# Weights in PSUM, and ScalarE scales the accumulator for half of the units of the first attention

## The chip, the cores and the metric

One core of one Trainium2 chip runs the whole program. The metric is the device time in microseconds (us). The engines are named as in the profile: PE (TensorE), PEld (its weight load), DVE (VectorE), ACT (ScalarE), POOL (GpSimd), SP (SyncE).

## The reference

A node feature matrix `x` (6250 nodes, 256 features) passes through four layers, each with a layer norm ahead of it and a residual around it: a graph attention with 4 heads, a mixture of 6 experts (2 chosen per node), a graph attention with 1 head, and a dense mixture of 8 experts. There are 106250 edges, sorted by their target `dst`. An attention computes:

```python
e = leaky_relu(a_src[src] + a_dst[dst], 0.2)     # per edge and head
m = segment_max(e, dst)
e = exp(e - m[dst])
alpha = e / segment_sum(e, dst)[dst]
out = segment_sum(alpha[:, :, None] * h[src], dst)
```

The dense mixture computes softmax shares of 8 experts for each node, three 256 x 256 layers per expert, and the sum of the experts' outputs weighted with the shares.

## The kernel before, in words

`attention(l, acc, sc)` runs once for each attention layer (`l` is 0 and 1; `H` heads, 4 and 1). Edges are cut into units of 256 (`UE`), each with targets in one tile of 125 nodes; a slot is 8 units (`U`), 16 columns of 128 edges (`Q`). There are 58 slots. The loop over slots is written out, five stages deep: in turn `i`, POOL gathers the rows of slot `i`, DVE builds the incidence of slot `i`, slot `i-1` has its maxima found, slot `i-2` has its weights computed and its units 0 to 3 summed, and slot `i-3` has its units 4 to 7 summed. Buffers `G` and `MB` have a ring of 3 slots.

POOL issues one indirect gather (L682) for each of the 16 columns; before a unit's two it waits until PE has summed that unit of three slots back (`summed`).

PE (from L686), per turn: two transposes (L729, L730) when the rows of slot `i-1` are there; `sums(3,4..6)`; two `spread` (L700, targets spread over partitions); `sums(3,7)`; the transposes of the selection (L741, L742); `sums(2,0..1)`; the product at L752; two more `spread`; `sums(2,2..3)`; the product at L765. A `sums(k,u)` (L715) is two matrix products of a unit's incidence with its rows, into one of four PSUM banks in turn; it waits until DVE has taken the sum four units back (`acc`).

ACT (from L771), per turn: copy of `LT` (L820), `place(0)` (L786, two operations that wait for `spread`), `hit(0)` (L798), the exponential of the weights (L828), `place(1)`, the selection copy (L835), `hit(1)`, eight small copies (L845), `place` and `hit` 2 and 3, and the exponential of the maxima's change, `c1` (L862). `lower` (L800) scales a tile of the accumulator `acc` with `c1`, one operation per head; it does so only for units that are not in `FUSED`, and before the change every unit is in it.

DVE (from L866), per turn: `dloc` (L965), logits and weights of slot `i-2` between the scan of slot `i-1` (L974 to L996, with `te` at L991), `scale(0)`, `merge(3,4)`, `merge(3,5)`, the rest of the selection (L1002), `scale(1)`, `merge(3,6)`, `merge(3,7)`, L1009 to L1018, `scale(2)`, the maxima (L1023 to L1056), `scale(3)`, and then `merge(2,0..3)` with four `incidence` (L952) among them. `scale` in layer 0 multiplies the gathered rows with the weights (L935); in layer 1 it multiplies the incidence with them (L938). `merge` of a unit in `FUSED` is one operation per head (L920): accumulator tile times `c1` plus PE's sum; of another unit it is one plain addition over all heads (L914), after `lowered`. Consecutive units may have the same tile, so both `merge` and `lower` wait for the sum of the unit before (`acc`).

`dense_experts` (L1070) runs over groups of 250 nodes (25 of them) and 8 experts `e`. PE does `layer2` of the expert before, `layer1` of this one, `layer3` of the one before; at `e == 5` it then transposes the shares of the next group (`turn_shares`, L1152), which waits for `cw`. DVE adds each expert's output to `X` (`collect`, L1360, after `layer3`) and computes the next group's shares: `shares` at `e == 4`, `normal_shares` (L1335 to L1341, makes `cw`) at `e == 5`, behind `collect`.

Of the kernel before, what the change touches and what calls it, by code (L numbers as in the profile page):

```python
# [18 lines left out]
F32 = mybir.dt.float32  # L19
I32 = mybir.dt.int32  # L20
BF16 = mybir.dt.bfloat16
ALU = mybir.AluOpType
# [3 lines left out]
P = 128  # L26
N = 6250
D = 256
TN = 125
# [4 lines left out]
C = 2  # L34
UE = P * C
UNITS = (E + (UE - 1) * NT) // UE
U = 8
# [20 lines left out]
HEADS = (4, 1)  # L58
FUSED = ((0, 1, 2, 3, 4, 5, 6, 7), (0, 1, 2, 3, 4, 5, 6, 7))
SLOPES = (0.2, 0.01)  # L60
# [7 lines left out]
def build(nc, a, out):  # L68
    ctx = ExitStack()
    with ctx:  # L70
        def sb(name, shape, dt=F32, scope=ctx):
            return scope.enter_context(nc.sbuf_tensor(name, shape, dt))
# [472 lines left out]
        def attention(l, acc, sc):  # L545
# [14 lines left out]
            if l == 1:  # L560
                qe = sb(p + "qe", [P, RING, Q], F32, sc)
                b = sb(p + "b", [P, RING, Q, H], F32, sc)
                wt = sb(p + "wt", [P, RING, Q, H], F32, sc)
                M = sb(p + "M", [P, MR, CP, TN], F32, sc)
# [35 lines left out]

            def sum_bank(u):
                return bank[(4, 5, 1, 7)[u % 4]]

# [29 lines left out]
            with nc.Block() as block:  # L633
# [53 lines left out]
                def _(pe):  # L687
                    def slot(i, r, t):
# [14 lines left out]
                        def sums(k, u):  # L703

                            if not has(i, k):
                                return
                            rk = (r - k) % RING
                            if u % 2 == 0:
                                pe.wait_ge(S(p + "scaled"), i * V - k * V + (u // 2 + 1))
                            if u >= 4 or late(i, k + 1):  # L710
                                after(pe, p + "acc", i * U - k * U + (u - 3))
                            for c in range(C):
                                q = u * C + c
                                left = MB[:, rk, q, :] if l == 0 else M[:, turn(r, k, u // 2), q % CP, :]
                                mm_ = nc.tensor.matmul(sum_bank(u)[0:TN, 0:HW], left, G[:, rk, q, :], start=(c == 0), stop=(c == C - 1))  # L715
                            mm_.then_inc(S(p + "summed"), 1)
# [26 lines left out]
                        sums(2, 0)  # L743
                        sums(2, 1)
                        if one:

                            pe.wait_ge(S(p + "MB"), i * V)
                            pe.wait_ge(S(p + "RS"), i)
                            if late(i, 2):
                                after(pe, p + "top", i - 1)  # L750
                            for q in range(Q):
                                mm_ = nc.tensor.matmul(V_ps[:, q * 3 * H:(q + 1) * 3 * H], hot(r1, q), RS[:, :, q, :], start=True, stop=True)  # L752
                            mm_.then_inc(S(p + "V"), 1)
                        spread(2)
                        spread(3)
                        sums(2, 2)
                        sums(2, 3)
                        if one:

                            pe.wait_ge(S(p + "rhs"), i)  # L760
                            pe.wait_ge(S(p + "MT"), i * V)
                            if late(i, 2):
                                after(pe, p + "xs", i - 1)
                            for q in range(Q):
                                mm_ = nc.tensor.matmul(Xe_ps[:, q * 6 * H:(q + 1) * 6 * H], MT[:, turn(r, 1, q // CP), q % CP, :],  # L765
                                                       rhs[:, q // C, :, 0:KM:KM - 1, :], start=True, stop=True)
                            mm_.then_inc(S(p + "Xe"), 1)
                    run(pe, slot)

                @block.scalar  # L770
                def _(act):  # L771
                    tile_regs = [[act.alloc_register(f"{p}atile{k}_{u}") for u in range(U)] for k in range(RING)]

                    def slot(i, r, t):
# [40 lines left out]
                        if one:  # L815
# [4 lines left out]
                            nc.scalar.copy(LT[:, :], rowT_ps[:, P:2 * P]).then_inc(S(p + "LT"), 1)  # L820
                        place(0)
                        lower(3, U - 2)
                        hit(0)
                        if two:

                            act.wait_ge(S(p + "te"), i - 1)
                            to = wt[:, r2, :, :] if l == 1 else G[:, r2, :, :].rearrange("p q (h w) -> p q h w", h=H)[:, :, :, DH]
                            nc.scalar.activation(to, te[:, :, :], ACT.Exp).then_inc(S(p + "w"), 1)  # L828
                        lower(3, U - 1)
                        place(1)  # L830
# [6 lines left out]
                        if one:  # L837
# [9 lines left out]
                            ins.then_inc(S(p + "ad_in"), 1)  # L847
                        lower(2, 0)
                        place(2)
                        lower(2, 1)  # L850
                        hit(2)
                        place(3)
                        lower(2, 2)
                        hit(3)
                        lower(2, 3)
                        lower(2, 4)
                        lower(2, 5)
                        if one:
# [7 lines left out]
                def _(v):  # L866
# [32 lines left out]
                    def slot(i, r, t):  # L899
# [3 lines left out]
                        def merge(k, u):  # L903
# [6 lines left out]
                            if u in own:  # L910
                                v.wait_ge(S(p + "lowered"), scaled_acc(k, i, u))
                                at = acc[:, bass.ds(j * HW, HW)]
                                ins = nc.vector.tensor_tensor(at, at, sum_bank(u)[0:TN, 0:HW], ALU.add)
                            else:  # L914
# [3 lines left out]
                                for h in range(H):  # L918
                                    at = acc[:, bass.ds(j * HW + h * W, W)]
                                    ins = nc.vector.scalar_tensor_tensor(at, at, c1[:, rk, u, h:h + 1], sum_bank(u)[0:TN, h * W:(h + 1) * W],  # L920
                                                                         ALU.mult, ALU.add)
                            ins.then_inc(S(p + "acc"), 1)

                        def scale(v_):
# [8 lines left out]
                            if l == 0:  # L933
                                g = G[:, r2, at, :].rearrange("p q (h w) -> p (q h) w", h=H)
                                ins = nc.vector.tensor_tensor(g[:, :, 0:DH], g[:, :, 0:DH], g[:, :, DH:W].broadcast_to([P, CP * H, DH]), ALU.mult)  # L935
                            else:
                                after(v, p + "summed", (i * V - 2 * V + v_) * 2 - 2 * MR + 2)
                                ins = nc.vector.tensor_tensor(M[:, turn(r, 2, v_), :, :], MB[:, r2, at, :], wt[:, r2, at, :].broadcast_to([P, CP, TN]), ALU.mult)  # L938
                            ins.then_inc(S(p + "scaled"), 1)
# [130 lines left out]
        def dense_experts(acc, sc):  # L1070
# [39 lines left out]
            with nc.Block() as block:  # L1110
# [173 lines left out]
                def _(v):  # L1284
# [655 lines left out]
```

## Time and profile before

| what | us |
|---|---|
| median of 3 runs | 4750.13 (4743.02 to 4752.10) |
| the profiled execution | 4749.81 |
| its span | 4748.1 |
| PE, DVE, ACT, POOL busy | 3401.8, 2688.4, 1539.8, 2214.1 |
| first attention: first to last gather | 184.6 to 1519.7 |
| second attention: first to last gather | 2346.5 to 3537.0 |
| dense experts | about 3590 to 4748 |

The span is one execution on the chip, from its first to its last instruction; the profiled execution's own time is 1.7 us above it. "Busy" is the time in which an engine had an instruction under way. Idle time of an engine matters only where it lies on the path that sets the end of a stage, so the stages are read one by one.

### The profile page before, as it was taken

The numbers are of one execution on the slowest core, as the hardware profiler recorded it, in microseconds if no ns is written. First come the engines' busy times: TensorE is split into PE (matmuls) and PEld (weight loads), VectorE is DVE, ScalarE is ACT, GpSimd is POOL, SyncE is SP. The second block draws the span as 40 slices with busy tenths as digits, with TensorE's granted clock in tenths as the row PEclk, the third lists the DMA queues.
The fourth block names the chain that finished last, engine by engine and source line by source line (L and its number), as shares of the span: only waits on it lengthen the run. The fifth ranks groups of instructions, "written<-read, shape, count | busy, mean of one in ns | idle before, by whom it ended". The sixth has DMA issues, their size and how long they took to land. (4 is left out here: it accounts for less than half of the span.)

```text
span 4748.1 us, 73243 instructions
## 1 busy us (share of the span) xinstructions
PE 3401.8 (72%) x16240; PEld 2620.6 (55%) x16241; DVE 2688.4 (57%) x8451; ACT 1539.8 (32%) x4325; POOL 2214.1 (47%) x2095
## 2 busy tenths in 40 slices
PE   5267667665776768884467766666558999999999
PEld 3144444444444557773245444444436888888887
DVE  7478888788887775555455556655555412222121
ACT  2233333333332203331133333333333333333333
POOL 0377777777776013227577777777750000000000
PEclk9676776777667559996667788888878999999999
DMA  3333333333336214443344444444461000000000
GB/s 100 80 95 93 94 94 95 95 94 94 93 94 78 90 34 158 157 132 102 95 105 106 106 105 105 106 106 105 106 84 57 7 5 6 4 6 6 4 7 7
DMA packets 382578, 369.58 MB, mean 78 GB/s; under 512 B 249324, under 2 KB 309388, under 8 KB 382242
## 3 DMA queue, kind: packets, MB, share of 16 engines
q0 software_dynamic: 107072, 272.84, 23.1%
q1 hardware_dynamic: 272774, 92.39, 8.1%
q14 instruction: 244, 2.00, 0.1%
q8 instruction: 92, 1.51, 0.1%
q10 hardware_dynamic: 2396, 0.84, 0.1%
HBM read 324.13 MB, written 41.59 MB: 77 GB/s over the span
## 5 line engine op out<-in xcount | busy, mean ns | idle before, releaser
L682 POOL DMA_INDIRECT g_G<-rows,g_pack x1856 | 1959.6, 1056 | 782.1 <-issue 496.4
L715 PE MATMUL bank<-g_G,g_MB 128*125 128x260 f32 x1856 | 718.4, 551 | 145.4 <-DVE acc L920 143.2
L786 ACT ACTIVATE g_mt_d<-bank,unode 125x256 bf16<-125x256 f32 x928 | 384.9, 465 | 898.5 <-PE bank L700 898.4
L715 PE MATMUL bank<-g_G,g_M 128*125 128x257 f32 x1856 | 612.8, 489 | 84.9 <-DVE acc L920 84.1
L715 PEld LDWEIGHTS bank<-g_G,g_MB 128*125 128x125 f32 x1856 | 486.4, 277 | 337.3 <-DVE g_G L935 152.0
L920 DVE SCALAR_TENSOR_TENSOR acc<-acc,g_c,bank 125x65 f32 (+1 forms) x2320 | 619.0, 316 | 88.9 <-DVE acc L920 83.3
L1360 DVE SCALAR_TENSOR_TENSOR X<-bank,e_cw,X 125x256 f32 (+1 forms) x400 | 175.2, 479 | 842.9 <-PE bank L1186 842.9
L1256 ACT ACTIVATE e_h<-bank,e_bi_c,e_sc_c 128x250 f32<-128x250 f32 x800 | 404.2, 556 | 556.8 <-PE bank L1177 419.7
L715 PEld LDWEIGHTS bank<-g_G,g_M 128*125 128x125 f32 x1856 | 441.4, 249 | 223.8 <-DVE g_M L938 89.6
L935 DVE TENSOR_TENSOR g_G<-g_G 128x1024 f32<-128x1024 f32 x232 | 283.1, 1221 | 191.4 <-ACT g_G L828 191.4
L1186 PE MATMUL bank<-e_w,e_h 128*125 128x256 f32 x1600 | 377.9, 379 | 3.1 <-ACT e_h L1256 3.1
L1177 PE MATMUL bank<-e_h,e_w 128*128 128x250 f32 x1600 | 376.6, 377 | 1.2 <-ACT e_h L1256 1.2
L1168 PE MATMUL bank<-e_xnT,e_w 128*128 128x250 f32 x1600 | 371.9, 374 | 0.0
L798 ACT ACTIVATE g_MT<-g_mt_d,ones 125x512 bf16<-125x512 bf16 x464 | 335.6, 723 | 11.3
L1186 PEld LDWEIGHTS bank<-e_w,e_h 128*125 128x125 f32 x1600 | 299.3, 187 | 47.2 <-ACT e_h L1256 3.9
L1168 PEld LDWEIGHTS bank<-e_xnT,e_w 128*128 128x128 f32 x1600 | 303.7, 190 | 36.3 <-issue 0.7
L1177 PEld LDWEIGHTS bank<-e_h,e_w 128*128 128x128 f32 x1600 | 296.1, 190 | 42.7 <-issue 8.0
L938 DVE TENSOR_TENSOR g_M<-g_MB,g_wt 128x500 f32<-128x500 bf16 x232 | 155.7, 671 | 288.8 <-PE bank L715 282.3
L952 DVE TENSOR_TENSOR g_MB<-iota_b,g_dloc 128x500 f32<-128x500 bf16 (+1 forms) x464 | 301.9, 673 | 0.1
L820 ACT COPY g_LT<-bank 64x128 f32<-64x128 f32 (+1 forms) x116 | 29.8, 257 | 804.9 <-PE bank L730 804.9
L729 PE MATMUL bank<-ident,g_b 128*16 128x128 f32 x58 | 21.6, 372 | 336.0 <-DVE g_dloc L965 265.7
L729 PE MATMUL bank<-ident,g_G 128*64 128x128 f32 x58 | 23.5, 405 | 317.7 <-DMA g_G<-rows,g_pack 317.7
(302 smaller groups left out, 4194.6 us busy)
## 6 DMA issues: line engine op xcount, KB each, us to landing
g_G<-rows,g_pack POOLq DMA_INDIRECT x1856
acc<-in_edge_attr SPq DMA_DIRECT2D x50, 531.2 KB
g_pack<-edge_pack SPq DMA_DIRECT2D x928, 2.0 KB
g_drow<-edge_dst SPq DMA_DIRECT2D x928, 1.0 KB
expert_out<-x_y SPq DMA_DIRECT2D x54, 256.0 KB
g_qe<-edge_q SPq DMA_DIRECT2D x464, 1.0 KB
rows<-acc SPq DMA_DIRECT2D x25, 253.9 KB
rows<-n_T SPq DMA_DIRECT2D x25, 251.0 KB
```

The source lines that it names most:

```text
L682: nc.gpsimd.indirect_dma_start(G[:, r, q, :], None, rows_d[l], bass.IndirectOffsetOnAxis(ap=pack[:, r, q, 0:1], axis=0)).then_inc(S(p + f" ...
L715: mm_ = nc.tensor.matmul(sum_bank(u)[0:TN, 0:HW], left, G[:, rk, q, :], start=(c == 0), stop=(c == C - 1))
L786: ins = nc.scalar.activation(mt_d[:, v_ % 2, k * C:(k + 1) * C, :], bank[2 + v_ % 2][0:TN, k * UE:(k + 1) * UE].rearrange("p (e c) -> p c ...
L798: nc.scalar.activation(MT[:, turn(r, 1, v_), :, :], mt_d[:, v_ % 2, :, :], ACT.Relu, bias=ones[0:TN, 0:1], scale=-1.0).then_inc(S(p + "MT" ...
L920: ins = nc.vector.scalar_tensor_tensor(at, at, c1[:, rk, u, h:h + 1], sum_bank(u)[0:TN, h * W:(h + 1) * W], ALU.mult, ALU.add)
L935: ins = nc.vector.tensor_tensor(g[:, :, 0:DH], g[:, :, 0:DH], g[:, :, DH:W].broadcast_to([P, CP * H, DH]), ALU.mult)
L952: nc.vector.tensor_tensor(MB[:, r, at, :], iota_b[:, 0:TN].unsqueeze(1).broadcast_to([P, CP, TN]), dloc[:, r, at, 0:1].broadcast_to([P, CP ...
L1168: mm = nc.tensor.matmul(bank[m][:, 0:GN], w1[:, e, k, m * P:(m + 1) * P], xnT[:, r, k, :], start=(k == 0), stop=(k == 1))
L1177: mm = nc.tensor.matmul(bank[2 + m][:, 0:GN], w2[:, e, k, m * P:(m + 1) * P], h1[:, k, :], start=(k == 0), stop=(k == 1))
L1186: mm = nc.tensor.matmul(bank[4 + u][0:TN, 0:D], h2[:, e % 2, k, u * TN:(u + 1) * TN], w3[:, e, k, :], start=(k == 0), stop=(k == 1))
L1256: ins = nc.scalar.activation((h1 if q == 0 else h2[:, e % 2, :, :])[:, m, :], bank[2 * q + m][:, 0:GN], ACT.Relu, bias=bi_c[:, q, m, e:e + ...
L1360: ins = nc.vector.scalar_tensor_tensor(xt, bank[4 + u][0:TN, 0:D], cw[:, r, u, e:e + 1], xt, ALU.mult, ALU.add)
```

## The change

- `FUSED` for layer 0 becomes units 0 to 3. Units 4 to 7 are scaled by ACT (`lower`, four operations of 65 columns) and added by DVE (one operation of 260 columns).
- The exponentials of the weights go into PSUM bank 7 (`w_ps`), and `scale` reads them there in both layers. Layer 0 also still writes them to column 64 of each head in `G`. The tile `wt` is gone.
- `sums` uses three banks in turn (4, 5, 1) in place of four, and waits for the sum three units back.
- PE's order: `sums(2,1)` moves behind the product at L752, `sums(2,3)` behind the one at L765.
- ACT's order: the exponential comes first after `LT`, then `lower(3,4)`, `place(0)`, `hit(0)`, `lower(3,5)`, `place(1)`, ...; `lower(3,6)` and `lower(3,7)` come behind the eight copies, ahead of `place(2)`. The calls `lower(2,...)`, which did nothing, are gone.
- In the dense experts `normal_shares` comes ahead of `collect` at `e == 5`.

```diff
-FUSED = ((0, 1, 2, 3, 4, 5, 6, 7), (0, 1, 2, 3, 4, 5, 6, 7))
+FUSED = (tuple(range(4)), tuple(range(8)))
...
-                wt = sb(p + "wt", [P, RING, Q, H], F32, sc)
...
-            def sum_bank(u):
-                return bank[(4, 5, 1, 7)[u % 4]]
+            w_ps = bank[7][:, 0:QH].rearrange("p (q h) -> p q h", h=H)
+
+            def sum_bank(r, k, u):
+
+                return bank[(4, 5, 1)[((r - k) % RING * U + u) % 3]]
...
-                            if u >= 4 or late(i, k + 1):
-                                after(pe, p + "acc", i * U - k * U + (u - 3))
+                            if u >= 3 or late(i, k + 1):
+                                after(pe, p + "acc", i * U - k * U + (u - 2))
...
                         sums(2, 0)
-                        sums(2, 1)
                         if one:
...
                             mm_.then_inc(S(p + "V"), 1)
+                        sums(2, 1)
                         spread(2)
                         spread(3)
                         sums(2, 2)
-                        sums(2, 3)
                         if one:
...
                             mm_.then_inc(S(p + "Xe"), 1)
+                        sums(2, 3)
...
+                        if two:
+
+                            act.wait_ge(S(p + "te"), i - 1)
+                            if l == 0:
+                                nc.scalar.activation(G[:, r2, :, :].rearrange("p q (h w) -> p q h w", h=H)[:, :, :, DH], te[:, :, :], ACT.Exp)
+                            nc.scalar.activation(w_ps, te[:, :, :], ACT.Exp).then_inc(S(p + "w"), 1)
+                        lower(3, 4)
                         place(0)
-                        lower(3, U - 2)
                         hit(0)
-                        if two:
-
-                            act.wait_ge(S(p + "te"), i - 1)
-                            to = wt[:, r2, :, :] if l == 1 else G[:, r2, :, :].rearrange("p q (h w) -> p q h w", h=H)[:, :, :, DH]
-                            nc.scalar.activation(to, te[:, :, :], ACT.Exp).then_inc(S(p + "w"), 1)
-                        lower(3, U - 1)
+                        lower(3, 5)
                         place(1)
...
-                        lower(2, 0)
+                        lower(3, 6)
+                        lower(3, 7)
                         place(2)
-                        lower(2, 1)
                         hit(2)
...
-                                ins = nc.vector.tensor_tensor(g[:, :, 0:DH], g[:, :, 0:DH], g[:, :, DH:W].broadcast_to([P, CP * H, DH]), ALU.mult)
+                                w = w_ps[:, at, :].rearrange("p q h -> p (q h)").unsqueeze(2).broadcast_to([P, CP * H, DH])
+                                ins = nc.vector.tensor_tensor(g[:, :, 0:DH], g[:, :, 0:DH], w, ALU.mult)
...
-                                ins = nc.vector.tensor_tensor(M[:, turn(r, 2, v_), :, :], MB[:, r2, at, :], wt[:, r2, at, :].broadcast_to([P, CP, TN]), ALU.mult)
+                                ins = nc.vector.tensor_tensor(M[:, turn(r, 2, v_), :, :], MB[:, r2, at, :], w_ps[:, at, :].broadcast_to([P, CP, TN]), ALU.mult)
...
                         for e in range(NX):
+                            if follows(i) and e == 5:
+                                normal_shares(i + 1, 1 - r)
                             if e or late(i, 1):
                                 collect(i if e else i - 1, r if e else 1 - r, i * NX + e - 1, (e - 1) % NX)
...
-                                if e == 5:
-                                    normal_shares(i + 1, 1 - r)
```

## Rows read from the trace of the kernel before

**Rows 1.** The page, part 1: busy us (share of the span) x instructions.
```profile
PE 3401.8 (72%) x16240; PEld 2620.6 (55%) x16241; DVE 2688.4 (57%) x8451; ACT 1539.8 (32%) x4325; POOL 2214.1 (47%) x2095
```

**Rows 2.** Busy time by stretch; columns in the first line; first attention, second, dense experts.
```profile
core 0: us, PE busy (x) PEld busy (x) DVE busy (x) ACT busy (x) POOL busy (x), PEclk, DMA share, GB/s
400.00:1400.00 1000.00, 664.03 (x3127) 450.14 (x3126) 813.61 (x2818) 328.26 (x1037) 788.98 (x693) 0.71 0.38 94
2500.00:3500.00 1000.00, 635.93 (x3515) 454.70 (x3516) 602.89 (x2057) 353.77 (x1172) 761.89 (x781) 0.81 0.45 105
3700.00:4700.00 1000.00, 962.96 (x4613) 835.99 (x4612) 217.91 (x593) 381.68 (x772) 0.00 (x0) 1.00 0.02 6
```

**Rows 3.** PE's waits, 3700 to 4700 us: waited for, us in total, times, longest us.
```profile
PE bank L1152 <- DVE e_cw L1341: 35.0, 22, 1.6
PE bank L1186 <- ACT e_h L1256: 2.0, 1, 2.0
```

**Rows 4.** POOL by line, 400 to 1400, then 2500 to 3500: busy, mean ns | idle before.
```profile
L682 POOL DMA_INDIRECT g_G<-rows,g_pack x693 | 789.9, 1140 | 211.3 <-issue 181.4 <-PE bank L715 29.9
...
L682 POOL DMA_INDIRECT g_G<-rows,g_pack x781 | 762.3, 976 | 238.2 <-issue 210.4 <-PE bank L715 27.8
```

**Rows 5.** The order of time, 813 to 819 us: start us, us, engine line op.
```profile
813.74 0.86 DVE L920 SCALAR_TENSOR_TENSOR acc<-acc,g_c,bank 125x65 f32 x4 [0.24 <-DVE acc L920]
813.86 0.95 POOL L682 DMA_INDIRECT g_G<-rows,g_pack  x1 [0.30 <-issue]
...
818.14 1.22 DVE L935 TENSOR_TENSOR g_G<-g_G 128x1024 f32<-128x1024 f32 x1
...
818.25 1.93 POOL L682 DMA_INDIRECT g_G<-rows,g_pack  x1 [0.30 <-issue]
```

**Rows 6.** The same for POOL: first and last of 154 lengthened gathers of that kind.
```profile
400.94 1.57 POOL L682 DMA_INDIRECT g_G<-rows,g_pack  x1 [0.30 <-issue]
...
1397.44 1.93 POOL L682 DMA_INDIRECT g_G<-rows,g_pack  x1 [0.30 <-issue]
```

**Rows 7.** DVE by line and form, whole span: busy us, mean ns | idle before.
```profile
L1883 DVE TENSOR_TENSOR x_y<-bank,xbo 128x512 f32<-128x512 f32 x54 | 37.0, 686 | 33.8 <-PE bank L1828 33.3 <-issue 0.4
...
L1526 DVE TENSOR_TENSOR r_y<-acc,r_den 125x256 f32 x40 | 15.2, 422 | 4.0 <-issue 3.3
```

**Rows 8.** DVE by line, 400 to 1400 us.
```profile
L935 DVE TENSOR_TENSOR g_G<-g_G 128x1024 f32<-128x1024 f32 x174 | 212.4, 1221 | 139.9 <-ACT g_G L828 139.9
L952 DVE TENSOR_TENSOR g_MB<-iota_b,g_dloc 128x500 f32<-128x500 bf16 x172 | 112.0, 672 | 0.0
```

**Rows 9.** The order of time of one slot, 807 to 829 us.
```profile
807.41 0.22 DVE L965 TENSOR_TENSOR g_dloc<-g_pack,ubase 128x64 f32<-128x64 f32 x1
...
808.78 0.23 DVE L991 TENSOR_TENSOR g_te<-g_xs 128x64 f32<-128x64 f32 x1
...
811.18 0.30 ACT L828 ACTIVATE g_G<-g_te 128x64 f32<-128x64 f32 x1
...
811.51 1.23 DVE L935 TENSOR_TENSOR g_G<-g_G 128x1024 f32<-128x1024 f32 x1 [1.85 <-ACT g_G L828]
...
817.65 0.35 DVE L1009 TENSOR_REDUCE g_adz<-g_rhs 125x64 f32<-125x192 bf16 x1
...
829.04 0.22 DVE L965 TENSOR_TENSOR g_dloc<-g_pack,ubase 128x64 f32<-128x64 f32 x1
```

**Rows 10.** ACT by line and form, whole span.
```profile
L1256 ACT ACTIVATE e_h<-bank,e_bi_c,e_sc_c 128x250 f32<-128x250 f32 x800 | 404.2, 556 | 556.8 <-PE bank L1177 419.7 <-PE bank L1168 137.1
...
L1501 ACT ACTIVATE r_rhT<-bank,r_br 128x250 f32<-128x250 f32 x25 | 11.7, 470 | 49.2 <-PE bank L1471 49.2
```

**Rows 11.** ACT by line, 400 to 1400 us.
```profile
L786 ACT ACTIVATE g_mt_d<-bank,unode 125x256 bf16<-125x256 f32 x348 | 144.3, 465 | 377.4 <-PE bank L700 377.4
L798 ACT ACTIVATE g_MT<-g_mt_d,ones 125x512 bf16<-125x512 bf16 x173 | 125.4, 725 | 4.2
L845 ACT COPY g_rhs<-g_tab 125x24 bf16 x344 | 42.5, 216 | 0.0
...
L835 ACT CAST g_RS<-bank 128x128 bf16<-128x128 f32 x43 | 11.2, 261 | 0.0
```

**Rows 12.** DVE by line, 2500 to 3500 us.
```profile
L938 DVE TENSOR_TENSOR g_M<-g_MB,g_wt 128x500 f32<-128x500 bf16 x196 | 131.5, 671 | 250.8 <-PE bank L715 250.8
```

More of the change, by code:

```diff
@@ L714, in sums @@
                                 left = MB[:, rk, q, :] if l == 0 else M[:, turn(r, k, u // 2), q % CP, :]
-                                mm_ = nc.tensor.matmul(sum_bank(u)[0:TN, 0:HW], left, G[:, rk, q, :], start=(c == 0), stop=(c == C - 1))
+                                mm_ = nc.tensor.matmul(sum_bank(r, k, u)[0:TN, 0:HW], left, G[:, rk, q, :], start=(c == 0), stop=(c == C - 1))
                             mm_.then_inc(S(p + "summed"), 1)
@@ L820, in slot @@
                             nc.scalar.copy(LT[:, :], rowT_ps[:, P:2 * P]).then_inc(S(p + "LT"), 1)
-                        place(0)
-                        lower(3, U - 2)
-                        hit(0)
                         if two:
                             act.wait_ge(S(p + "te"), i - 1)
-                            to = wt[:, r2, :, :] if l == 1 else G[:, r2, :, :].rearrange("p q (h w) -> p q h w", h=H)[:, :, :, DH]
-                            nc.scalar.activation(to, te[:, :, :], ACT.Exp).then_inc(S(p + "w"), 1)
-                        lower(3, U - 1)
+                            if l == 0:
+                                nc.scalar.activation(G[:, r2, :, :].rearrange("p q (h w) -> p q h w", h=H)[:, :, :, DH], te[:, :, :], ACT.Exp)
+                            nc.scalar.activation(w_ps, te[:, :, :], ACT.Exp).then_inc(S(p + "w"), 1)
+                        lower(3, 4)
+                        place(0)
+                        hit(0)
+                        lower(3, 5)
                         place(1)
@@ L847, in slot @@
                             ins.then_inc(S(p + "ad_in"), 1)
-                        lower(2, 0)
+                        lower(3, 6)
+                        lower(3, 7)
                         place(2)
-                        lower(2, 1)
                         hit(2)
                         place(3)
-                        lower(2, 2)
                         hit(3)
-                        lower(2, 3)
-                        lower(2, 4)
-                        lower(2, 5)
                         if one:
@@ L912, in merge @@
                                 at = acc[:, bass.ds(j * HW, HW)]
-                                ins = nc.vector.tensor_tensor(at, at, sum_bank(u)[0:TN, 0:HW], ALU.add)
+                                ins = nc.vector.tensor_tensor(at, at, sum_bank(r, k, u)[0:TN, 0:HW], ALU.add)
                             else:
@@ L919, in merge @@
                                     at = acc[:, bass.ds(j * HW + h * W, W)]
-                                    ins = nc.vector.scalar_tensor_tensor(at, at, c1[:, rk, u, h:h + 1], sum_bank(u)[0:TN, h * W:(h + 1) * W],
+                                    ins = nc.vector.scalar_tensor_tensor(at, at, c1[:, rk, u, h:h + 1], sum_bank(r, k, u)[0:TN, h * W:(h + 1) * W],
                                                                          ALU.mult, ALU.add)
```

## The prediction

> **What bounds the kernel now.** I read the page first. No engine is busy over the whole span: PE is at 72%, DVE at 57%, POOL at 47% [rows 1]. So I asked for three stretches of 1000 us, one inside each stage that the diff touches: first attention, second attention, dense experts [rows 2].
>
> In the dense experts PE is busy 963 of 1000 us at full granted clock: that stage is PE, and each idle us of PE there is a us of the kernel. Its waits have one large entry, the transpose of the shares at L1152, which waits 1.6 us for `cw` once per group of 250 nodes, 22 times in the stretch, 35.0 us [rows 3].
>
> In both attentions POOL is the bound. It is busy 789 and 762 us, and the rest is the 0.30 us before each gather: 693 gathers with 211 us before them, 781 with 238 us, which fills both stretches [rows 4]. A slot has 16 gathers, so a slot takes 1000 x 16 / 693 = 23.1 us in the first and 1000 x 16 / 781 = 20.5 us in the second. (Cut by PE's row transposes, the first has 43.35 slots per 1000 us; I use 23.07.) The gather is the same instruction in both, yet means 1.14 us in one and 0.98 us in the other. The order of time shows why. A gather that begins during the scaled sum L920 takes 0.95 us. One that begins 0.11 us into the scaling L935 takes 1.93 us: it ends 0.82 us after L935 does [rows 5]. I laid all 692 gathers that start in the stretch against the DVE operation under way at their start. Of 167 in an L935, 154 are longer than 0.98 us, together 95 us above the 0.95 floor (the first and last of them are [rows 6]); of 72 in an L952 all 72, together 37 us; of 184 in an L920 none. L935 and L952 have two tensor inputs in SBUF; L920 has its second one in PSUM. In the second attention the same count gives 15 us for L938 and 7 us for L952.
>
> The Trainium skill (SBUF — State Buffer, Who interferes with whom) says that a DVE instruction with two SBUF inputs contends with a GpSimd instruction that reads SBUF and that the later one blocks, and it infers elsewhere in that section that `tensor_tensor` does not stall descriptor generation. The rows here agree with the first sentence and not with the second. By the second, the PSUM operand would free nothing; that is rival 3 below.
>
> **Part 1, weights in PSUM, first attention.** Four L935 per slot read the weight from PSUM. By the L920 rows this frees POOL: 95 us per 43.35 slots = 2.2 us per slot. POOL's own limit becomes 23.07 - 2.2 = 20.9 us. The scaling itself should cost the same: 512 columns with a PSUM operand take 686 ns (L1883) [rows 7], 500 with both in SBUF 672 ns (L952) [rows 8]. The exponential is now done twice (once into column 64 of each head, for the sums' weight column, and once into PSUM); the second costs about 0.2 us on ACT (0.30 us, less the 0.09 by which ACT's operations overlap) [rows 9].
>
> **Part 2, exponential ahead.** DVE waits for the exponential 139.9 us in 43 slots, 3.23 us each [rows 8], because ACT places it behind `place(0)` and `hit(0)`, which wait for PE. `te` is ready 1.6 us after the slot's first DVE operation (807.41 to 808.78 + 0.23) and L935 starts at 811.51 [rows 9]. Now it comes first: `w` is there at about 1.6 + 0.5 = 2.1, and DVE reaches `scale(0)` at 2.24 anyway. This wait goes to zero. It was slack under POOL's bound, so it is no gain by itself; it is room.
>
> **Part 3, hand-offs between ACT and DVE.** Units 4 to 7 of a slot: DVE's four scaled sums of 65 columns become one sum of 260, and ACT scales before it. `lower(3,u)` waits for the sum of unit u-1 and the sum of u waits for `lower(3,u)`, so the two engines take turns. Price of one `lower`: nearest is an ACTIVATE with a scale taken from a tile. L1256 (250 columns, scale and bias tiles) means 556 ns and L1501 (250 columns, bias tile alone) 470 ns [rows 10], so the scale tile adds 0.09 us. L786 at 256 columns is busy 144.3 / 348 = 0.415 us each, a pair 0.83 us, its second starting 0.37 us behind the first [rows 11]; less 191 columns at about 1 ns that is 0.17, with the tile 0.26 us between starts, and 0.35 us for the last. Four heads: 3 x 0.26 + 0.35 = 1.13 us, and 1.04 until ACT's next starts. Without the 0.09 it would be 0.77; I take 1.13, because L1256 and L1501 differ in that alone. The sum of 260 is 0.43 us by L1526 (256 columns, 422 ns) [rows 7]. ACT's other pieces: `place` 0.84, `hit` 0.72 (0.64 until the next starts), the eight copies 42.5 / 43 = 0.99, the selection copy 0.26 [rows 11].
>
> ACT's order from the start of a slot (DVE's L965 = 0): `w` starts at 1.84; lower 4 from 2.05; place(0) 3.09; hit(0) 3.96; lower 5 4.60 to 5.73; place(1) 5.64; selection copy 6.39; hit(1) 6.56; copies 7.20; lower 6 8.10 to 9.23; DVE's sum of unit 6 9.26 to 9.69; lower 7 9.72 to 10.85; DVE's sum of unit 7 10.88 to 11.31. DVE's L1009 follows at 11.25. From there nothing in the slot changes: L1009 at 817.65 to the next slot's L965 at 829.04 is 11.39 us [rows 9]. The slot by this chain is 22.6 us. In between DVE idles some 3.5 us, which part 2 has made room for; its work falls only by about 4 x 0.4 us (0.86 for four scaled sums [rows 5] against 0.43). So the bound passes from POOL (20.9) to the turn-taking chain (22.6): 58 slots x (23.07 - 22.6) = **27 us**. With `lower` at 0.77 us the four of them take 1.4 us less: 21.2, or 108 us.
>
> **Part 4, PE's order and three banks.** Sums of a slot now use three banks in turn, so each waits for the sum three units back, and bank 7 holds the weights. `sums(3,7)` now waits for DVE's unit 4, at about 3.9, and the selection transpose is queued behind it: ready at about 5.9, before ACT is free to copy it (6.39). `sums(2,1)` waits for unit 6 (9.7), `sums(2,2)` for unit 7, `sums(2,3)` for unit 0 of the next slot back, which is why it moved behind the transposed product at L765. PE has 664 / 43.35 = 15.3 us of work per slot [rows 2] against 22.6; next slot's first transpose can start at about 19.5 of this slot, its first spread ends near 2.5, before place(0) needs it at 3.1. I cost this at nothing; the cover is 0.6 us. Were PE a fifth slower in the some 6 us before its first spread, place(0) would come 0.6 us late, and about half of that would land on each slot (PE's own start moves with it): +0.3 us a slot, 17 us. POOL waits for `summed` of three slots back, and the latest of these now has 6 us or more in hand.
>
> **Part 5, second attention.** L938 gets its PSUM operand: its share of the lengthening is 15 us per 49 slots, 0.3 us per slot, 18 us in 58. No `lower` there. DVE has idle time to give (it waits 250.8 us before L938 in the stretch [rows 12]). But L952 is then reached some 0.8 us earlier in the slot, against a fixed rhythm of gathers of 1.25 us, and now happens to miss most of them: at the rate of the first attention (37 us in 43 slots) it would take 0.85 us per slot rather than 0.14. So -18 to +23 us; I take **-5**.
>
> **Part 6, dense experts.** The three small operations behind `cw` move ahead of the accumulation that waits for L1186. Their input `ex` is ready by then (a whole layer pass of PE, about 4 us, lies between). The transpose at L1152 waits for nothing: 24 groups x 1.59 = **38 us**; nothing else of PE's waits there is over 2 us [rows 3]. PE then is 100% busy at a clock that is already full.
>
> **Sum.** 4749.8 (the profiled run; span 4748.1) - 27 - 5 - 38 = 4680; the median of the runs, 4750.1, is 0.3 above the profiled run, so **4680 us**.
>
> **Rivals.** (1) Turns cheaper than priced: `lower` at 0.77 us, so the chain is 21.2 and POOL's 20.9 nearly shows: 4750 - 108 - 38 - 5 = 4599. For: 65 columns are short and L845's small copies start 0.12 us apart. Against: the pair L1256/L1501. (2) Turns dearer, the slower side: the four scalings of a unit do not overlap (4 x 0.35 = 1.4, that is +0.27 each for four) and each of seven hand-offs takes 0.12 us instead of 0.03: 22.6 + 1.08 + 0.63 = 24.3 us a slot, +72 us, so 4750 + 72 - 38 - 5 = 4779. It decides from a slot of 23.07 + 43/58 = 23.8 us on. For: they read and write the same tile at an address from a register, and no row shows that on ACT. Against: L786's pairs overlap, and DVE started 0.03 us after ACT's end at 811.48 [rows 9]. (3) The PSUM operand does not free POOL: the lengthening stays, POOL stays at 23.07, and only part 6 is left: 4712. Against: 184 gathers in L920.
>
> **Chances.** Forecast (4650 to 4740, with the second attention going either way) 0.55, rival 1 0.20, rival 3 0.13, rival 2 0.12. The range 4590 to 4750 leaves out rival 2 and rival 1 with the second attention at its best. What a measurement tells from no change is about 0.2%, 9.5 us. Faster needs under 4740.6: 0.84. Within: 0.06, the near side of rival 2. Slower: 0.10.
>
> **What the next profile would show.** Gathers that start in L935 and L938 at 0.95 us; the L935 wait on the exponential gone; L920 split into scaled sums of 65 and plain sums of 260 near 0.43 us; ACT's new group at about 0.29 us busy each; DVE waiting on ACT before the sums of units 5, 6 and 7, 3 to 4 us per slot; POOL with real waits on L715, busy near 75%; L1152 without a wait. I am wrong if POOL is still saturated in the first attention, if ACT's four scalings are far from 1.1 us, or if PE waits before L700 or L741.

## The result, and the profile after

The changed kernel takes 4666.8 us (median of 4 runs, 4660.5 to 4670.5), the kernel before 4747.9 us (4 runs, 4743.0 to 4752.1). The ratio is 0.983, 95% interval 0.981 to 0.985: 1.7% faster. The forecast was 4680 us, with 4590 to 4750 as its range. The profiled execution took 4670.5 us, its span is 4668.8.

The same three stretches as [rows 2], columns as there:

```profile
400.00:1400.00 1000.00, 703.82 (x3207) 453.60 (x3205) 757.38 (x2373) 515.77 (x1817) 708.97 (x712) 0.67 0.39 97
2500.00:3500.00 1000.00, 654.04 (x3509) 427.70 (x3508) 597.06 (x2041) 357.80 (x1172) 757.75 (x777) 0.75 0.47 105
3650.00:4650.00 1000.00, 998.00 (x4791) 872.60 (x4791) 229.36 (x615) 396.20 (x803) 0.00 (x0) 1.00 0.02 6
```

In the first attention POOL is busy 709 us rather than 789, ACT 516 rather than 328. The second is nearly what it was. In the dense experts PE went from 963 to 998 us at full granted clock.

POOL by line, in the first and then the second attention (compare [rows 4]); and PE's largest wait in the dense experts (compare [rows 3]):

```profile
L684 POOL DMA_INDIRECT g_G<-rows,g_pack x712 | 709.3, 996 | 291.0 <-issue 182.2 <-PE bank L717 108.8
...
L684 POOL DMA_INDIRECT g_G<-rows,g_pack x777 | 757.8, 975 | 239.6 <-issue 180.4 <-PE bank L717 59.2
```

```profile
PE bank L1186 <- ACT e_h L1256: 2.0, 1, 2.0
```

A gather of the first attention now means 996 ns instead of 1140, and POOL has begun to wait for PE: 291 us idle before 712 gathers, where 0.30 us each would be 214. It is no longer the bound there: a slot in this stretch takes 1000 x 16 / 712 = 22.47 us, where it took 23.09 (693 gathers). In the second attention almost nothing moved (976 to 975 ns). PE's wait at L1152 is gone.

Where the time went, by the start of the first and the last gather of each attention in the order of time. "Lengthened" is the sum of what the 928 gathers of an attention took above 0.95 us; "a slot" is the row above it divided by 58:

| stretch | before, us | after, us | difference |
|---|---|---|---|
| first attention, first to last gather | 1335.1 | 1289.7 | -45.4 |
| of it a slot | 23.02 | 22.24 | -0.78 |
| lengthened there | 173 | 47 | |
| from there to the second attention's first gather | 826.8 | 832.4 | +5.7 |
| second attention, first to last gather | 1190.5 | 1189.6 | -0.9 |
| lengthened there | 27 | 27 | |
| last gather to the end | 1211.1 | 1172.4 | -38.7 |

The last gather isn't the end of an attention: its rows still have to be summed. The first DVE operation behind the last sum, before and then after:

```profile
1573.45 0.34 DVE L1515 TENSOR_SCALAR r_den<-acc 125x200 f32<-125x200 f32 x1 [1.12 <-PEq L88]
...
1533.92 0.34 DVE L1515 TENSOR_SCALAR r_den<-acc 125x200 f32<-125x200 f32 x1 [1.12 <-PEq L88]
```

It comes 39.5 us earlier, so the first attention gained 39.5 us. Of the 45.4, 5.9 us are gathers that now run further ahead of the sums (the last one by 59.6 us in place of 53.8), and they come back as the 5.7 us of the next row. From L1515 to the second attention's first gather it is 773.0 us before and 772.8 after.

What a slot of the first attention consists of now can be read off the order of time; one slot, ACT and DVE only:

```profile
813.11 0.22 DVE L965 TENSOR_TENSOR g_dloc<-g_pack,ubase 128x64 f32<-128x64 f32 x1
...
814.91 0.26 ACT L828 ACTIVATE bank<-g_te 128x64 f32<-128x64 f32 x1
...
815.11 0.99 ACT L814 ACTIVATE acc<-acc,g_c  x4
815.28 1.21 DVE L935 TENSOR_TENSOR g_G<-g_G,bank 128x1024 f32<-128x1024 f32 x1
...
817.48 1.05 ACT L814 ACTIVATE acc<-acc,g_c  x4
...
818.74 0.42 DVE L912 TENSOR_TENSOR acc<-acc,bank 125x260 f32 x1 [1.92 <-ACT acc L814]
...
820.80 1.07 ACT L814 ACTIVATE acc<-acc,g_c  x4
...
822.09 0.43 DVE L912 TENSOR_TENSOR acc<-acc,bank 125x260 f32 x1 [1.30 <-ACT acc L814]
...
822.64 1.07 ACT L814 ACTIVATE acc<-acc,g_c  x4 [0.76 <-DVE acc L912]
...
823.92 0.42 DVE L912 TENSOR_TENSOR acc<-acc,bank 125x260 f32 x1 [1.40 <-ACT acc L814]
824.26 0.35 DVE L1009 TENSOR_REDUCE g_adz<-g_rhs 125x64 f32<-125x192 bf16 x1
```

The scaling L935 follows the exponential at once. Then three sums of 260 columns (units 5, 6, 7) each wait 1.3 to 1.9 us for ACT, and ACT itself waits 0.76 us for the sum of unit 6. L1009 comes 11.15 us after L965; the forecast had 11.25. Over 1000 us of the first attention (400 to 1400) DVE waits this much:

```profile
DVE acc L912 <- ACT acc L814: 182.6, 117, 2.3
DVE acc L912 <- PE bank L717: 22.2, 15, 1.9
DVE g_RS L1002 <- ACT g_RS L838: 12.3, 43, 0.5
```

182.6 us in 44.5 slots is 4.1 us of waiting for ACT in each slot.

### The profile page after: what moved, and what is told of

Read it like the earlier page. It is cut to its first block and busy times, and to the rows that moved or that the text cites. A ratio compares the mean times of both kernels' runs of the same rounds, so it can differ in the third digit from the quotient of the medians.

```text
span 4668.8 us, 74055 instructions
## 1 busy us (share of the span) xinstructions
PE 3444.0 (74%) x16240; PEld 2577.2 (55%) x16241; DVE 2584.1 (55%) x7755; ACT 1779.4 (38%) x5311; POOL 2079.9 (45%) x2095
## 5 line engine op out<-in xcount | busy, mean ns | idle before, releaser
L684 POOL DMA_INDIRECT g_G<-rows,g_pack x1856 | 1830.0, 986 | 868.6 <-issue 460.8
L717 PE MATMUL bank<-g_G,g_MB 128*125 128x260 f32 x1856 | 738.1, 549 | 301.0 <-DVE acc L912 225.1
L717 PEld LDWEIGHTS bank<-g_G,g_MB 128*125 128x125 f32 x1856 | 462.7, 270 | 471.7 <-DVE acc L912 200.2
L717 PE MATMUL bank<-g_G,g_M 128*125 128x257 f32 x1856 | 634.7, 489 | 20.7 <-DVE acc L919 20.6
L717 PEld LDWEIGHTS bank<-g_G,g_M 128*125 128x125 f32 x1856 | 418.6, 241 | 147.9 <-DVE acc L919 26.2
L919 DVE SCALAR_TENSOR_TENSOR acc<-acc,g_c,bank 125x65 f32 (+1 forms) x1392 | 419.8, 343 | 119.5 <-PE bank L717 73.4
L952 DVE TENSOR_TENSOR g_MB<-iota_b,g_dloc 128x500 f32<-128x500 bf16 (+1 forms) x464 | 302.1, 673 | 0.1
L935 DVE TENSOR_TENSOR g_G<-g_G,bank 128x1024 f32<-128x1024 f32 x232 | 280.7, 1210 | 0.5 <-ACT bank L828 0.5
L814 ACT ACTIVATE acc<-acc,g_c x928 | 243.4, 335 | 54.8 <-DVE acc L912 47.5
L912 DVE TENSOR_TENSOR acc<-acc,bank 125x260 f32 x232 | 97.7, 421 | 273.8 <-ACT acc L814 244.2
```

Source lines behind the costliest of these rows:

```text
L684: nc.gpsimd.indirect_dma_start(G[:, r, q, :], None, rows_d[l], bass.IndirectOffsetOnAxis(ap=pack[:, r, q, 0:1], axis=0)).then_inc(S(p + f" ...
L717: mm_ = nc.tensor.matmul(sum_bank(r, k, u)[0:TN, 0:HW], left, G[:, rk, q, :], start=(c == 0), stop=(c == C - 1))
L814: ins = nc.scalar.activation(at, at, ACT.Copy, scale=c1[:, rk, u, h:h + 1])
L952: nc.vector.tensor_tensor(MB[:, r, at, :], iota_b[:, 0:TN].unsqueeze(1).broadcast_to([P, CP, TN]), dloc[:, r, at, 0:1].broadcast_to([P, CP ...
```

## The experiments

The question was which of the change's parts made the 45 us, and whether the turns of ACT and DVE (each waits for the other's last result, unit after unit) now set the slot. All figures are from one profiled execution each, with the kernel before run beside it, unless an interval is given.

### 1. The dense experts alone

The kernel before, with this edit only:

```diff
                         for e in range(NX):
+                            if follows(i) and e == 5:
+                                normal_shares(i + 1, 1 - r)
                             if e or late(i, 1):
...
-                                if e == 5:
-                                    normal_shares(i + 1, 1 - r)
```

> The kernel before with one edit of the change: the shares' three operations ahead of the accumulation in the dense experts. Theory: the transpose at L1152 no longer waits, 24 groups x 1.59 us = 38 us less than before (about 4710), from the last gather to the end 1211 becomes 1173 us, and the wait of 35.0 us per 1000 us is gone; both attentions stay at 1335 and 1190 us from first to last gather. Rival: PE without pauses there falls to a lower granted clock and gives part of it back; then less than 38 us.

It took 4711.1 us, the kernel before beside it 4748.9: 37.8 less. From the last gather to the end it is 1172.6 us, and PE in the stretch of [rows 2] is as in the changed kernel:

```profile
3700.00:4700.00 1000.00, 998.00 (x4790) 872.24 (x4788) 226.59 (x607) 396.39 (x801) 0.00 (x0) 1.00 0.02 6
```

The granted clock stays at 1.00; nothing is given back. This part is settled. (The first attention was 1340.6 us here and 1335.1 us in the kernel before, with the same code there: differences under some 6 us in that row say nothing.)

### 2. No turns: all units fused again

```diff
-FUSED = (tuple(range(4)), tuple(range(8)))
+FUSED = (tuple(range(8)), tuple(range(8)))
```

> The changed kernel with all eight units of the first attention fused again (DVE scales and adds, ACT scales nothing); weights in PSUM, three banks, new orders stay. Theory: the turns of ACT and DVE set the 22.24 us of a slot. Without them POOL's own limit shows, 20.05 us of gathers and 0.85 us of lengthening by L952, about 20.9 us, DVE's own work being 19.84 us: first to last gather about 1212 us rather than 1290, the run about 4590 us. Rival: PE's order and its three banks set the slot; then 1290 us and 4668 us stay.

It took 4563.7 us: 103 less than the changed kernel, and 26 less than even the theory had. The first attention takes 1187.8 us, 20.48 a slot. The same kernel once more, with four runs:

> The changed kernel with all units fused once more, timed in rounds: 4564 us again, 3.9% below before, first attention 1188 us from first to last gather. If that one look was an outlier, it goes back towards 4590, the value first expected.

It took 4557.9 us (4 runs, 4553.7 to 4569.7), ratio to before 0.959, interval 0.956 to 0.962. The title's other half, ACT scaling the accumulator, therefore costs about 100 us of what the rest of the change gains. POOL, and DVE's largest wait, of the first execution, 400 to 1300 us:

```profile
L684 POOL DMA_INDIRECT g_G<-rows,g_pack x706 | 685.9, 971 | 215.1 <-issue 193.8 <-PE bank L717 21.3
```

```profile
DVE g_RS L1002 <- ACT g_RS L838: 35.3, 44, 1.8
```

POOL is saturated again (685.9 + 215.1 of 900 us), at 20.48 us a slot: 20.05 for gathers of 0.95 + 0.30 us and 0.43 for L952, which lengthens by 27 us in 58 slots rather than the 50 us assumed. DVE is as full: 818 of 900 us busy, and 68 us waiting (L1002 above, and 32.4 us of L919 for the L919 before it). PE's new order and its three banks are kept in this kernel, so they don't set 22.24 us; that rival falls. From here on this is "kernel 2".

### 3. One head scaled instead of four

```diff
-                            for h in range(H):
+                            for h in range(1):
                                 at = acc[:, bass.ds(j * HW + h * W, W)]
                                 ins = nc.scalar.activation(at, at, ACT.Copy, scale=c1[:, rk, u, h:h + 1])
```

Three of four heads' scalings of units 4 to 7 are left out.

> The changed kernel in which ACT scales one of four heads only (three quarters of the scaling of units 4 to 7 are left out). Theory: each scaling of a unit is about 0.35 instead of 1.05 us, four of them lie on the turn-taking chain, so the chain falls by 2.8 us from 22.24 to 19.4 us and POOL's limit of about 20.9 us shows: 1212 us from first to last gather, the run about 4590 us. Rival, PE's order and banks set the slot: 1290 us stays. Rival, the hand-offs' own latency rather than the scaling: a fall of under 1 us a slot, above 1240 us.

It took 4589.4 us; the first attention 1218.0 us, 21.00 a slot, with 57 us lengthened by L952: again 20.05 plus the lengthening, POOL's limit. ACT's scaling of a unit, and what DVE still waits for it, 400 to 1300 us:

```profile
L814 ACT ACTIVATE acc<-acc,g_c x171 | 56.6, 331 | 33.9 <-DVE acc L912 32.9
```

```profile
DVE acc L912 <- ACT acc L814: 128.0, 124, 3.9
```

One scaling is 0.33 us, and with 2.9 us less of it on the turns' chain the slot falls until POOL stops it. DVE still waits 3 us a slot (128.0 us in 43 slots); as POOL is never idle beyond its 0.30 us, these waits don't set the slot.

### 4. Weights in SBUF again, turns kept

```diff
+                wt = sb(p + "wt", [P, Q, H], F32, sc)
...
-                            if l == 0:
-                                nc.scalar.activation(G[:, r2, :, :].rearrange("p q (h w) -> p q h w", h=H)[:, :, :, DH], te[:, :, :], ACT.Exp)
-                            nc.scalar.activation(w_ps, te[:, :, :], ACT.Exp).then_inc(S(p + "w"), 1)
+                            to = wt[:, :, :] if l == 1 else G[:, r2, :, :].rearrange("p q (h w) -> p q h w", h=H)[:, :, :, DH]
+                            nc.scalar.activation(to, te[:, :, :], ACT.Exp).then_inc(S(p + "w"), 1)
...
-                                w = w_ps[:, at, :].rearrange("p q h -> p (q h)").unsqueeze(2).broadcast_to([P, CP * H, DH])
+                                w = g[:, :, DH:W].broadcast_to([P, CP * H, DH])
...
-                                ins = nc.vector.tensor_tensor(M[:, turn(r, 2, v_), :, :], MB[:, r2, at, :], w_ps[:, at, :].broadcast_to([P, CP, TN]), ALU.mult)
+                                ins = nc.vector.tensor_tensor(M[:, turn(r, 2, v_), :, :], MB[:, r2, at, :], wt[:, at, :].broadcast_to([P, CP, TN]), ALU.mult)
```

ACT also does one exponential less here in the first attention.

> The changed kernel with the weights read from SBUF again, in both attentions (one exponential into column 64 in the first, a tile in the second); everything else stays. Theory: gathers that begin in L935 and L938 are lengthened again, the first attention goes back to POOL's limit of about 23.0 us a slot, 1335 us from first to last gather (45 more than the changed kernel), the run about 4712 us. Rival: the PSUM operand does nothing and the first attention's gain is from the orders; then the gathers stay near 0.95 us and the first attention at 1290 us or, with one exponential less, 1278 us.

It took 4677.1 us, with 1302.5 us in the first attention: neither side's number. POOL is saturated again,

```profile
L685 POOL DMA_INDIRECT g_G<-rows,g_pack x711 | 783.5, 1102 | 216.6 <-issue 203.8 <-PE bank L718 12.8
```

and the lengthening is back, so the mechanism holds; but it adds up to 142 us, not 173. 221 gathers begin in an L935 and lose 0.40 us each, where in the kernel before 214 did and lost 0.58. What a gather loses depends on how far into the DVE operation it begins, and that has shifted: 0.68 us into it on average here, 0.47 in the kernel before. The worth of the PSUM operand beside the turns is 13 us only, because the turns' chain at 22.24 stands right under POOL's 22.46.

### 5. Weights in SBUF, no turns

Both edits of 2 and 4.

> All eight units fused, the weights in SBUF again in both attentions, new orders and three banks kept. With the turns gone POOL's limit shows, and this run tells what the weights in PSUM are worth. Theory: gathers that begin in L935 are lengthened, between 89 and 129 us in the first attention as in the two runs with SBUF weights so far, so 20.05 + 0.85 + 1.5 to 2.2 = 22.4 to 23.1 us a slot, 1300 to 1340 us from first to last gather against 1188 with the weights in PSUM; the run 4675 to 4715 us. Rival: the early exponential alone made the gain and the PSUM operand is worth the 13 us that it was worth beside the turns: about 1200 us and 4577 us.

It took 4691.5 us; the first attention 1323.1 us, 22.81 a slot, 163 us lengthened. Against kernel 2 the PSUM operand is worth 135 us in the first attention alone (the exponential that falls away here can only have made that less). One pair from the order of time:

```profile
813.04 1.22 DVE L935 TENSOR_TENSOR g_G<-g_G 128x1024 f32<-128x1024 f32 x1
813.14 1.93 POOL L685 DMA_INDIRECT g_G<-rows,g_pack  x1 [0.30 <-issue]
```

This kernel has the early exponential, the three banks and the new orders, and is 12 to 17 us faster in the first attention than the kernel before (1323 against 1335 and, in experiment 1, 1341). All of that is less lengthening (163 us against 173 and 178): POOL is saturated in all three, and those parts by themselves shorten nothing else.

### 6. L952 freed too

L952 still has two operands in SBUF. A copy of its first, the row of node numbers, goes into the free part of bank 7:

```diff
+            iota_ps = bank[7][:, 2 * P:2 * P + TN]
...
+                    nc.vector.tensor_copy(iota_ps, iota_b[:, 0:TN]).then_inc(S(p + "iota"), 1)
+                    v.wait_ge(S(p + "iota"), 1)
...
-                            nc.vector.tensor_tensor(MB[:, r, at, :], iota_b[:, 0:TN].unsqueeze(1).broadcast_to([P, CP, TN]),
+                            nc.vector.tensor_tensor(MB[:, r, at, :], iota_ps.unsqueeze(1).broadcast_to([P, CP, TN]),
```

First beside the turns, where theory says it is worth nothing in one attention and all in the other:

> The changed kernel with the row of node numbers, the first operand of L952, copied once into PSUM, so that L952 too has one tensor input in SBUF. Theory: the first attention is set by the turns, so freeing POOL there gives nothing: 1290 us stays although its lengthening (48 us) goes; in the second attention POOL is the bound and L952 is all of its lengthening (28 us): 1190 becomes about 1163 us, the run about 4640 us. Rival: a broadcast operand from PSUM does not free POOL; both stay.

It took 4639.0 us. The first attention stays at 1288.9 us although its lengthening fell from 47 to 1 us; the second goes from 1189.6 to 1162.2 us. In the first the freed time has become waiting for PE, here over 1000 us:

```profile
POOL g_G L685 <- PE bank L718: 141.7, 106, 3.2
```

In the changed kernel it was 108.8 us. That is what a bound elsewhere looks like.

Then without the turns:

> All units fused and L952's first operand in PSUM. Theory: no DVE operation of any length has two SBUF inputs then, a gather takes 0.95 + 0.30 us, a slot 20.05 us in both attentions: 1163 us from first to last gather in each, 4564 - 25 - 25 = about 4515 us. Rival: DVE, busy 898 of 1000 us in the first attention and waiting about 0.9 us a slot, is the next bound: then the first attention stays at 1180 us or more and the run ends near 4535 us.

It took 4531.8 us (4 runs, 4525.6 to 4533.9), ratio to before 0.953, interval 0.951 to 0.956: the fastest kernel of this case, 2.9% below the changed one. The second attention is at the bare limit, 1162.7 us, 20.05 a slot. The first is at 1183.9 us, as the rival said: gathers are short, and POOL waits.

```profile
L685 POOL DMA_INDIRECT g_G<-rows,g_pack x704 | 666.0, 946 | 234.9 <-issue 187.0 <-PE bank L718 48.0
```

```profile
DVE g_RS L1005 <- ACT g_RS L839: 35.2, 43, 1.8
DVE acc L922 <- DVE acc L922: 31.7, 129, 0.6
```

DVE is busy 818 of 900 us there and waits 35.2 + 31.7 us, together 885 us, while POOL now has 20 us more of idle time than its 0.30 us a gather. By these rows DVE is the next bound; no run that can be compared tests it. Kernel 2 already had DVE as full (818 + 68 of 900 us) and the same number of gathers (706 in 900 us, 704 here), so in its first attention POOL and DVE were at their limits together, and freeing L952 brought only 3 to 4 us there.

### 7. Two questions that stayed open

What the early exponential is worth once POOL is free (all units fused, exponentials put back behind `hit(0)`), and whether ACT could scale unit 4 alone at no cost (`FUSED` with all units but 4, without and with the edit of 6):

> All eight units fused, weights in PSUM, with the exponentials back behind place(0) and hit(0) as in the kernel before. Theory: that wait was slack while POOL took 23 us a slot and is none at 20.5; DVE has about 0.9 us of idle time a slot left, the late exponential costs it about 1.9 us or more, so the slot is about 21.5 us, 1245 us from first to last gather, the run about 4620 us. Rival: the early exponential gave nothing, the PSUM operand all; then 1188 us and 4562 us stay.

> The changed kernel with ACT scaling unit 4 alone (units 5 to 7 fused again): the one scaling that DVE has no need to wait for, since its tile is ready at the start of the slot. Theory: the waits of the turns and not the scaling cost the time, so POOL's limit shows as with all units fused, 20.5 us a slot, 1188 us from first to last gather, the run about 4562 us; no wait before the sum of 260 columns. Rival: 1.04 us more on ACT ahead of place(0) delays the slot by itself; then 1210 to 1250 us.

> ACT scaling unit 4 alone, and L952's first operand in PSUM. With all units fused and that operand in PSUM the first attention took 20.41 us a slot, set by DVE. Theory: DVE saves 0.43 us a slot here without a wait, so POOL's bare limit of 20.05 us shows: 1163 to 1170 us from first to last gather and a run of about 4515 us. Rival: DVE only waits longer for ACT before L1002 (0.8 us a slot with all fused), and the first attention stays at 1184 us or above, the run at 4532 us or above.

> The kernel with all eight units fused, weights in PSUM and the exponentials behind place(0) and hit(0), once more, because in the first look the kernel before itself took 5261 us and waits on issue and on nothing that the trace names filled both attentions (slots of 25 and 26 us in all three kernels). Where the kernel before takes about 4750 us: theory, the slot of the first attention is about 21.5 us, 1245 us from first to last gather, since DVE has 0.9 us idle a slot and the late exponential costs it 1.9 us or more; rival, 1188 us, the early exponential gave nothing.

These four were run on two other chips than experiments 1 to 6, on which the kernel before itself took 5261 and 5219 us, and they can't be set beside the others: 5175 and 5146 us for the late exponential, 5164 for unit 4 alone, and for unit 4 with L952 freed a ratio to before of 0.980, interval 0.977 to 0.983. The first attention took 1464 to 1471 us in the first two kernels and 1450 in the third, the second 1509 to 1525 us in all, so a slot has 25 us and more, beyond any limit found above. What set it is open. The row of SP's eight `drow` transfers looks like a lead, first in the late-exponential kernel there (slot of 25.2 us), then in kernel 2:

```profile
803.44 15.74 SPq L668 DMA_DIRECT2D g_drow<-edge_dst  x8
```

```profile
806.18 9.56 SPq L668 DMA_DIRECT2D g_drow<-edge_dst  x8
```

But such a row runs from the start of the first of eight issues to the end of the last, with SP's waits for `spread` between them. A single issue of L668 takes 237 ns in the median in both (the means are 243 and 246 ns), so SP has no more work there; it waits longer between, which may as well follow from the longer slot as cause it. Both questions are open.

## Why the prediction was right, point by point

- **What bounds the kernel.** Right in all three stretches. POOL saturated in both attentions, lengthened by DVE operations with two SBUF operands, PE in the dense experts.
- **Part 1, weights in PSUM.** The mechanism is right: 221 gathers of the first attention begin in an L935 of the changed kernel, and none is lengthened. The scaling costs 1210 ns with the PSUM operand, 1221 before. POOL's own limit was mis-sized: 20.9 us forecast, 20.48 measured (experiment 2), since the share of L952 was taken as a constant 0.85 us a slot and was 0.43 there. The same mistake stood in the expectation of experiment 4.
- **Part 2, exponential ahead.** The wait on it went from 139.9 us to nothing among DVE's waits, and by itself it gave little (experiment 5). Its worth in the freed kernel was not measured.
- **Part 3, the turns.** The bound did pass from POOL to the chain: 22.6 us a slot forecast, 22.47 measured in the middle of the stage (712 gathers in 1000 us); the 22.24 of the table is lower because it spreads the stage's start over all slots. In part this closeness is luck: two errors cancel in the slot's first part. In the slot shown above `lower(3,6)` starts 7.69 us after L965 (820.80 - 813.11), where 8.10 was forecast: `lower` was priced at 1.13 us and takes 1.05 in the mean of all, and two of them come before that point. But a hand-off was priced at 0.03 us. Over 1000 us, DVE's sum starts 0.21 us behind the end of `lower` (median of 132 that waited), and `lower` 0.13 us behind the end of the sum (44). From `lower(3,6)` to the sum of unit 7 that makes 3.12 us where 2.78 was forecast, and L1009 comes at 11.15 rather than 11.25. The other 0.15 us lie in the part that was to stay as it is: from L1009 to the next L965 it is 11.24 us in the median, not 11.39. Nearly all of it is one operation, before and after, that nothing in the change touches:

```profile
L1047 DVE CAST g_rhs<-g_lk 125x64 bf16<-125x64 f32 x43 | 15.4, 359 | 1.5
...
L1047 DVE CAST g_rhs<-g_lk 125x64 bf16<-125x64 f32 x45 | 9.9, 220 | 1.6
```

  In total the first attention gained 39.5 us by the time of L1515, against 27 forecast. The 0.62 us a slot in the middle (23.09 to 22.47) make 36 of them, where 0.47 was forecast; the other 4 fall in the first and last slots. DVE's idle time was put at some 3.5 us a slot; it is 4.1 + 0.5 on L912; the sum of 260 columns is 421 ns (0.43 forecast). Experiments 2 and 3 show that it is this chain and not PE's order that sets the slot.
- **Part 4, PE.** Cost nothing, as assumed: kernel 2 has the same order and banks and runs at POOL's limit.
- **Part 5, second attention.** -5 forecast, -0.9 measured, and for the reason given: L938's 13 us are gone and L952's went from 9 to 27 us. Another 4 us that are gone weren't L938's: 18 gathers of the kernel before were lengthened that began up to 0.28 us behind the end of the `memset` at L931.
- **Part 6, dense experts.** 38 us forecast, 38.7 measured, 37.8 alone.
- **Sum.** -70 forecast, -79 between the profiled executions and -81 by the medians. Of the 79, the first attention has 39.5 up to its last sum (12 more than forecast), the second 0.9 (4 less), the dense experts 38.7 (1 more).
- **Rivals.** Rival 3, the PSUM operand frees nothing, is refuted by experiment 5. Of rival 2, scalings without overlap are refuted: four take 1.05 us, one 0.335; its dearer hand-offs were real, 0.21 and 0.13 us, more than the 0.12 that it gave. Rival 1 had the right side but the wrong size for a scaling.

What the prediction did not do is price the change's parts against each other. Its own numbers, POOL's limit of 20.9 us and a chain of 22.6, say that the turns cost 1.7 us a slot, some 100 us in all; experiment 2 measures 102 us. Both limits were too high there, POOL's by 0.4 us and the chain's by 0.1 to 0.4, so the size of that difference owes something to luck; its sign doesn't.

## What to carry to other kernels

Where a queue of indirect gathers on GpSimd is the bound, look at the spread of one instruction's duration and at what VectorE was doing when the long ones began; moving one operand of a long VectorE operation to PSUM gave 135 us of one attention here, without making any instruction of GpSimd or VectorE cheaper by itself. Ask who waits for work that is handed to an idle engine: here a unit's scaling of 1.05 us saved VectorE 0.43 us of its own work and cost it up to 1.9 us of waiting. And when two edits go in together, set the limit that each leaves against the other's: the higher of the two limits is what shows.

## What the runs showed of the hardware

- A gather that begins within a VectorE operation with two SBUF operands is held up, and one that is under way when such an operation begins isn't. In the first attention of the kernel before, all 199 lengthened gathers that began in an L935 ended 0.81 to 0.83 us after it (1.93 us in the pair 813.04/813.14 above, and in [rows 5]), and of 147 during which an L935 began none was lengthened. With one operand of L935 and of L952 moved to PSUM (experiment 6), no gather that began in either was lengthened: a gather means 946 ns in the last kernel there, against 1126 ns in experiment 5 and 1140 before. The PSUM operand may be a broadcast and slows nothing (1210 and 1221 ns; L955, which is L952 with the PSUM operand, 670 and 672 ns).
- VectorE pays too: the cast L1047 takes 354 to 359 ns in the mean in the four kernels with the weights in SBUF and 199 to 227 in the five with them in PSUM. Its code is the same in all; what lengthens it wasn't tested.
- A hand-off between engines hasn't one price: DVE's L935 started 0.03 us behind the end of ACT's L828 in the kernel before (43 cases), its sum L912 0.21 us behind the end of `lower` in the changed one.
- ScalarE in place on a tile at an address from a register, 125 x 65 with a scale from a tile: 335 ns each, 0.24 us between starts. The Trainium skill (ScalarE: Activation LUTs, What ACT_TABLE_LOAD costs) gives 186 ns + 0.833 ns a column, 93 ns more for a pointer operand and an overlap of 93 ns. An estimate by these figures of the Trainium skill is 333 ns and 0.24 us, and the trace agrees.
- The lengthening is not a constant of the code: the same four L952 lengthened an attention by 7 to 57 us (experiment 1's second attention, experiment 3's first). By how far into a DVE operation the gathers begin (experiment 4) that is a matter of where in the gathers' rhythm of 1.25 us it falls; nobody moved it on purpose.
